# Attention over head pairs: the next pair's four query chunks in steps 0, 2, 4 and 6 instead of 0 to 3

## The reference

```python
q = (x @ wq).reshape(b, s, H, QH).transpose(0, 2, 1, 3)
q_nope, q_pe = (q[..., :NOPE], q[..., NOPE:])
...
q_pe = _rope(q_pe, cos, sin)
qs = jnp.concatenate([q_nope, q_pe], axis=-1)
ks_ = jnp.concatenate([k_nope, jnp.broadcast_to(k_pe, (b, H, s, ROPE))], axis=-1)
scores = jnp.einsum('bhqd,bhkd->bhqk', qs, ks_) * scale
scores = jnp.where(causal, scores, jnp.finfo(scores.dtype).min)
attn = jax.nn.softmax(scores, axis=-1)
out = jnp.einsum('bhqk,bhkd->bhqd', attn, v)
```

## Time and profile before

| | |
|---|---|
| median of 3 runs | 1463.27 us (1458.16 to 1464.06) |
| profiled execution: time, span | 1465.05 us, 1463.3 us |
| mean granted TensorE clock | 0.919 |
| busy over the span | PE 1235.1, POOL 1043.6, DVE 744.3, ACT 700.5 us |

### The profile page before, as it was taken

The page is one execution under the profiler, slowest core; times in us unless marked ns, Lnnn a source line. Parts: engine busy times, 40 slices in busy tenths (PEclk is TensorE's granted clock), DMA queues, the critical chain, the costliest instruction groups (busy, mean ns, idle before and its releaser), DMA issues. The chain is left out here.

```text
span 1463.3 us, 19068 instructions
## 1 busy us (share of the span) xinstructions
PE 1235.1 (84%) x5880; PEld 894.6 (61%) x5881; DVE 744.3 (51%) x1423; ACT 700.5 (48%) x1197; POOL 1043.6 (71%) x764
## 2 busy tenths in 40 slices
PE   6974699999992489988998897689889988998797
PEld 5863455555552356666666666556667666766686
DVE  4578522222224456544655464646546555563557
ACT  3221223333230356676667664246767676666242
POOL 2025768888874578888889876668988898876554
PEclk9986699999995689999999999879999999999999
DMA  9358345455555000000000000000000000002001
GB/s 326 116 157 210 97 62 83 79 79 81 80 75 166 8 8 8 8 1 8 8 8 1 0 1 12 8 8 8 2 7 8 8 8 1 0 1 60 5 8 51
DMA packets 66511, 68.30 MB, mean 47 GB/s; under 512 B 15072, under 2 KB 59680, under 8 KB 66304
## 3 DMA queue, kind: packets, MB, share of 16 engines
q1 hardware_dynamic: 48336, 43.42, 10.0%
q0 software_dynamic: 15168, 20.72, 9.1%
q10 hardware_dynamic: 2928, 3.15, 0.7%
HBM read 46.17 MB, written 21.10 MB: 46 GB/s over the span
## 5 line engine op out<-in xcount | busy, mean ns | idle before, releaser
L1531 POOL TENSOR_TENSOR att_prob_lo<-att_prob,att_prob_hi 128x1024 fp32r<-128x1024 f32 (+1 forms) x160 | 346.2, 2164 | 118.6 <-ACT att_prob_hi L1456 118.5
L1572 DVE TENSOR_REDUCE att_peak<-all_bank 128x1 f32<-128x512 f32 (+3 forms) x384 | 209.3, 551 | 245.4 <-PE all_bank L1343 175.8
L1359 PE MATMUL all_bank<-att_q_hl,sequence_k_hl 128*128 128x512 f32 (+1 forms) x960 | 267.9, 390 | 0.0
L1382 PE MATMUL all_bank<-att_prob_hi,sequence_v_hl 128*128 128x512 f32 (+1 forms) x640 | 212.9, 415 | 61.4 <-POOL att_prob_lo L1531 46.7
L1449 ACT ACTIVATE att_prob<-all_bank 128x1024 f32<-128x1024 f32 (+1 forms) x160 | 150.6, 941 | 156.8 <-PE all_bank L1365 155.0
L1359 PEld LDWEIGHTS all_bank<-att_q_hl,sequence_k_hl 128*128 128x128 f32 x960 | 175.0, 197 | 27.9
L1340 PE MATMUL all_bank<-sequence_k_hl,att_q_hl 128*128 128x512 f32 (+3 forms) x384 | 174.3, 457 | 5.7 <-DVE att_peak L1572 5.3
L1382 PEld LDWEIGHTS all_bank<-att_prob_hi,sequence_v_hl 128*128 128x128 f32 x640 | 113.1, 201 | 78.0 <-POOL att_prob_lo L1531 51.7
L1456 ACT CAST att_prob_hi<-att_prob 128x1024 fp32r<-128x1024 f32 (+1 forms) x160 | 154.2, 964 | 5.1
L916 PE MATMUL all_bank<-early_w_gu,moe_xgT 128*128 x316 | 148.8, 553 | 3.5 <-issue 2.4
L881 POOL DMA_INDIRECT sums<-moe_y,early_slot_far x79 | 125.5, 1588 | 36.4 <-issue 20.4
(11 more groups left out here) (246 smaller groups left out, 2164.2 us busy)
## 6 DMA issues: line engine op xcount, KB each, us to landing
sequence_w_raw<-wqk_rows SPq DMA_DIRECT2D x16, 256.0 KB, 2.6
early_w_gu<-in_gate SPq DMA_DIRECT2D x16, 224.0 KB, 5.5
early_w_gu<-in_up SPq DMA_DIRECT2D x16, 224.0 KB, 6.0
early_w_down<-in_down SPq DMA_DIRECT2D x1, 3584.0 KB, 19.6
sums<-early_zero SPq DMA_DIRECT2D x18, 128.0 KB, 3.7
all_xT<-in_xT SPq DMA_DIRECT2D x4, 512.0 KB, 8.5
all_x_tok<-in_x SPq DMA_DIRECT2D x1, 2048.0 KB, 16.4
x_rows<-all_x_tok SPq DMA_DIRECT2D x4, 512.0 KB, 3.0
```

The costliest lines, as they stand in the source:

```text
L1359: nc.tensor.matmul(ps, k_hl[:, ks, j * P:(j + 1) * P], q_hl[n % 2][:, qs, :, i * BW + q0:(i + 1) * BW], start=g == 0, stop=False)
L1382: mm = nc.tensor.matmul(out, v_hl[:, vs, j, :], part[:, u % 3, half * WIDE:half * WIDE + 2 * w].rearrange("p (h m) -> p h m", h=2), start= ...
L1531: nc.gpsimd.tensor_tensor(prob_lo[:, u % 3, 0:w], prob[:, u % 2, 0:w], prob_hi[:, u % 3, 0:w].bitcast(F32), ALU.subtract).then_inc(lo_sb, 1)
L1572: nc.vector.tensor_reduce(peak[:, n % 2, part, t // 2, h, t % 2:t % 2 + 1], piece_ps[y % 2][:, 0:w], AX_X, ALU.max).then_inc(peak_sb, 1)
```

## The change

The query chunks of the next pair stand in steps 0, 2, 4, 6. So that each piece still comes after its query chunk, the pair leaves 8 of its 24 pieces (not 3) to its own steps 0 to 3, and does 16 of the next pair's, in steps 4 to 9. The splitting of the weights moves from steps 4 and 5 to 7 and 8, DVE's `invert` and POOL's `product` move by a step or more, and the product of a pair's third block moves to step 0 of the next pair.

```diff
-    NEXT_PIECES = [0, 0, 1, 2, 3, 3, 3, 3, 3, 3]
-    OWN_PIECES = [2, 1] + [0] * (NG - 2)
-    FIRST_PIECES = [3, 3, 2] + [0] * (NG - 3)
-    EARLY = NP - sum(FIRST_PIECES)
-    INVERT_AT = {1: (-1, 0), 2: (-1, 1), 3: (0, 0), 4: (0, 1), 5: (1, 0), 6: (1, 1), 7: (2, 0), 8: (2, 1)}
-    PRODUCT_AT = {3: -1, 5: 0, 7: 1, 9: 2}
+    QUERY_AT = {0: 0, 2: 1, 4: 2, 6: 3}
+    NEXT_PIECES = [0, 0, 0, 0, 1, 3, 1, 3, 4, 4]
+    OWN_PIECES = [2, 3, 2, 1] + [0] * (NG - 4)
+    EARLY = NP - sum(OWN_PIECES)
+    INVERT_AT = {0: [(-1, 0)], 1: [(-1, 1)], 3: [(0, 0), (0, 1)], 5: [(1, 0)], 7: [(1, 1)], 8: [(2, 0)], 9: [(2, 1)]}
+    PRODUCT_AT = {0: -2, 2: -1, 4: 0, 8: 1}
...
-                    made = n + 1 < PAIRS and x < QC
+                    made = n + 1 < PAIRS and x in QUERY_AT
...
-                        q_high(n + 1, x)
+                        q_high(n + 1, QUERY_AT[x])
                     if x in last_of:
                         sums(n, last_of.index(x))
-                    if x == 4 and n + 2 < PAIRS:
+                    if x == 7 and n + 2 < PAIRS:
                         weights_high(n + 2)
...
-                        if 1 <= x <= QC:
-                            q_low(n + 1, x - 1)
-                        if x < QC:
-                            rotate(n + 1, x)
+                        if x - 1 in QUERY_AT:
+                            q_low(n + 1, QUERY_AT[x - 1])
+                        if x in QUERY_AT:
+                            rotate(n + 1, QUERY_AT[x])
...
+                product(PAIRS * NB - 2)
```

More of the change, by code:

```diff
@@ L1253, in phase_attention @@
     block_needs = [1 + max(y for y in range(NP) if pieces[y][0] // 2 == i) for i in range(NB)]
-    NEXT_PIECES = [0, 0, 1, 2, 3, 3, 3, 3, 3, 3]
-    OWN_PIECES = [2, 1] + [0] * (NG - 2)
-    FIRST_PIECES = [3, 3, 2] + [0] * (NG - 3)
-    EARLY = NP - sum(FIRST_PIECES)
-    INVERT_AT = {1: (-1, 0), 2: (-1, 1), 3: (0, 0), 4: (0, 1), 5: (1, 0), 6: (1, 1), 7: (2, 0), 8: (2, 1)}
-    PRODUCT_AT = {3: -1, 5: 0, 7: 1, 9: 2}
+    QUERY_AT = {0: 0, 2: 1, 4: 2, 6: 3}
[4 more added lines that the diff above has]
+    PRODUCT_AT = {0: -2, 2: -1, 4: 0, 8: 1}
     def aside(n, x):
[L1264 to L1267, removed]
+        out = [("query", n + 1, QUERY_AT[x])] if n + 1 < PAIRS and x in QUERY_AT else []
+        out += [("piece", n, EARLY + sum(OWN_PIECES[:x]) + a) for a in range(OWN_PIECES[x])]
         if n + 1 < PAIRS:
@@ L1484, in _ @@
                     n, x, _, _ = at(u)
-                    made = n + 1 < PAIRS and x < QC
+                    made = n + 1 < PAIRS and x in QUERY_AT
                     if made:
-                        swap(n + 1, x)
+                        swap(n + 1, QUERY_AT[x])
                     if u + AHEAD < STEPS:
@@ L1546, in _ @@
                     if n + 1 < PAIRS:
-                        if 1 <= x <= QC:
-                            q_low(n + 1, x - 1)
-                        if x < QC:
-                            rotate(n + 1, x)
+                        if x - 1 in QUERY_AT:
+                            q_low(n + 1, QUERY_AT[x - 1])
+                        if x in QUERY_AT:
+                            rotate(n + 1, QUERY_AT[x])
                     if u + AHEAD < STEPS:
                         low(u + AHEAD)
-                    if x == 5 and n + 2 < PAIRS:
+                    if x == 8 and n + 2 < PAIRS:
                         weights_low(n + 2)
@@ L1616, in _ @@
                         beside(item)
-                    if x in INVERT_AT:
-                        i, half = INVERT_AT[x]
+                    for i, half in INVERT_AT.get(x, ()):
                         if n * NB + i >= 0:
```

## The result

The changed kernel takes 1467.38 us (median of 20 runs, 1459.56 to 1475.14), the kernel before on the same chips 1461.39 us (20 runs, 1452.17 to 1464.23). The ratio is **1.0044 [1.0024, 1.0064]**: no gain, but a small loss. The forecast was 1453, with a range of 1437 to 1467. The profiled execution took 1467.2 us with a span of 1465.4 and a mean granted clock of 0.924.

The account below looks back on a forecast made before the run. PE sets the pace, held up in two gaps per middle pair by `sums`. Gains of 22.1 + 1.0 - 0.6 = 22.5 us, less 12.0 for clock drops, net 10.5: 1453 us as run median, range 1437 to 1467.

Parts of the forecast that it names:

- what holds PE up: Middle pairs: gaps of 0.62 us (step 1) and 3.35 (step 3) wait for `sums`, behind `q_high` on ACT.
- Rival (e): Step 3's gap doesn't move because POOL's `low` was its cause: 1477 us, chance 0.03.
- what step 2 gains: Without `q_low` ahead of step 2's rotation, `values` of step 3 starts 2.01 us sooner; its gap becomes 1.9.
- the same chain behind it: Step 0's chain from query to `values` of step 1 stays; only cover goes, so step 1's gap becomes 1.9 us.
- the moved `invert` costs nothing: DVE: moved `invert` priced at nothing, since DVE has 21 us free in a pair and it is read steps later.
- the old loss of 1.71 goes: Middle pairs: the 1.71 us lost to the lower clock behind step 3's gap is gained if new gaps keep the clock.
- The terms for steps 2 to 9: Per middle pair: step 2 gains 2.01 us; steps 4 to 9 lose 2.80 to two queries, gain 0.92 from fewer piece columns.
- a sign of being wrong: Among the listed signs against the forecast: PEclk of 0.5 behind step 1's gap.
- The edge that I took between 1.98 and 2.12 us: Gap length at which the clock falls: 1.98 us kept it, 2.12 lost it; gaps of about 1.9 lie there.
- first and last pairs: First pairs gain 0.5 us each; last pairs lose 0.3 each, idle PE taking most of 1.15 us of added pieces.
- (a) to (c): No gap loses the clock, 1441 (0.26); every step 3 gap does, 1465 (0.18); both of each pair, 1485 (0.05).
- (d): POOL becomes the bound from step 4 on, step 0's query waiting for the weights: about 1467 us, chance 0.10.

Follow-up runs that it names:

- the reduction: Changed kernel with ACT's `sums` ahead of `q_high`, and `att_whole` as a reduction over one operand instead of a maximum of two: 1416.47 us, 0.9688 of the kernel before.
- the run with its gap filled: Kernel before with nine thrown-away matmuls of 512 columns ahead of `values` in step 3: 1442.14 us, 0.9873 of the kernel before.
- the fastest kernel: Changed kernel with `sums` ahead of `q_high`, `att_whole` as a reduction, and own pieces 3, 3, 2 in steps 0 to 2: 1416.04 us, 0.9683.
- the kernel with step 1's gap filled: Changed kernel with six thrown-away matmuls of 512 columns ahead of `values` in step 1: 1462.84 us, 1.0007 of the kernel before.

## Why the prediction was wrong

**Right: what holds PE up.** Both gaps wait for `sums` behind `q_high`, and the view's releaser for step 3, POOL's `low`, was misleading. With `sums` ahead of `q_high` both gaps of the changed kernel fall below 0.5 us and its time goes from 1.0044 to 0.9742 of the kernel before, `low` being untouched. Rival (e) falls.

**Right: what step 2 gains.** From `values` of step 1 to that of step 3 it was 596.89 - 584.33 = 12.56 us before and is 787.51 - 777.01 = 10.50 in the undisturbed pair: 2.06 sooner, where 2.01 was forecast. The step 3 gap is 1.79, where 1.9 was.

**Failed: that step 0 keeps "the same chain behind it", and that the moved `invert` costs nothing.** Step 0's own chain, on which both gaps rest, grew. From the query to `values` of step 1 it was 584.33 - 576.20 = 8.13 us and is 728.59 - 720.13 = 8.46. DVE, then POOL, in the changed kernel at that place:

```profile
719.88 0.16 DVE L1580 TENSOR_TENSOR att_whole<-att_peak 128x4 f32<-128x4 f32 x1
720.08 2.78 DVE L1584 SCALAR_TENSOR_TENSOR att_minus<-all_bf,att_whole 128x512 bf16<-128x512 bf16 x1
722.78 0.94 DVE L1595 RECIPROCAL att_rden<-att_den 128x128 f32<-128x128 f32 x1
723.64 0.62 DVE L1571 TENSOR_REDUCE att_peak<-all_bank 128x1 f32<-128x512 f32 x1
724.18 0.67 DVE L1565 TENSOR_TENSOR all_xT<-all_bank,sequence_cst_turned 128x512 f32<-128x512 f32 x1
```

```profile
719.89 2.40 POOL L1529 TENSOR_TENSOR att_prob_lo<-att_prob,att_prob_hi 128x1024 fp32r<-128x1024 f32 x1 [0.40 <-ACT att_prob_hi L1454]
723.15 1.29 POOL L1503 TENSOR_TENSOR all_xT<-all_xT,sequence_cst_turned 128x512 f32<-128x512 f32 x1 [0.85 <-ACT all_xT L1427]
724.93 1.28 POOL L1506 TENSOR_TENSOR all_xT<-all_xT 128x512 f32<-128x512 f32 x1 [0.49 <-DVE all_xT L1565]
```

The moved pieces bring the third block's maximum to this place. `att_whole` finds POOL free (0.16 us), then `att_minus` starts at 720.08, when POOL's `low` is running until 722.29, and takes 2.78 us; before, all 14 behind an `att_whole` in 540 to 860 us took 0.69. In the changed kernel the 13 there average 1.97. Behind it stands the moved `invert` (0.94), then a peak, and so `by_cos` ends only at 724.85. POOL's second rotation needs it and stands idle for 0.49; 0.33 of that arrive at `values`, whose gap is 2.2 and not 1.9. Putting the `invert` back gave these 0.33 back in the profile, so that part is shown. That `att_minus` is long by POOL's `low` is argued from the rows; the same wait is shown for `att_whole`, by the reduction. The step failed by looking at DVE's 21 free us, which are a sum over the pair: what counted was its queue over the 5 us ahead of `by_cos`, and that its instructions can wait for POOL's.

**Mis-sized: "the old loss of 1.71 goes".** An undisturbed pair is 46.91, forecast 46.14, 0.77 longer. The chain is 0.33 of it. Most of the rest, 0.4, is this term: by the granted clock a drop in the kernel before cost 1.71 us, by the run with its gap filled 1.3. Why it cost less than the granted clock makes of it stays open. The terms for steps 2 to 9, 2.01 - 2.80 + 0.92 = 0.13, held: with the `invert` put back and no drop the changed kernel's pair is 46.58, the filled one's of before 46.66. The new row of waits is small: pieces in step 8 wait 0.3 us for a peak (0.29 at 714.12; the forecast was no gap over 0.5, and one of 12 is 0.6). By the rows DVE takes them late behind another `att_minus`; that wasn't tried by itself.

**Near in number, by luck, and wrong in place: the clock.** I gave nine drops, half of the 14 gaps of step 3 and two in the first pairs. There are 10, but seven stand behind step 1's gap in the middle pairs, which the prediction had named as a sign of being wrong. That I gave none for that gap rested on its coming out below 2 us; the longer chain made it 2.2. Step 3's 1.79 lost nothing in the middle pairs. The edge that I took between 1.98 and 2.12 us isn't there: gaps of 2.20 to 2.22 kept the clock five times, one of 1.79 in a first pair lost it. The 2.12 stood in a stretch where PE was busy for 0.52 of 2.50 us, and so said little of a gap in dense work. The price of a drop: a pair with one is 48.4 to 48.5 us long for 46.9, so 1.5 to 1.6, where 1.71 was used (48.8 in one that also waits 0.3 us longer for a peak).

**Mis-sized: first and last pairs.** First pairs were to gain 0.5 each and lost 1.62 and 0.28. The last two pairs of a batch together went from 78.7 to 81.5 us; about 2.2 of it is the last pair, forecast 0.3. Its idle PE was to swallow most of 1.15 us of added pieces; yet PE's gaps there are as long as before (2.8 us in sum), so the pieces came on top. The other us stays open.

In sum the attention phases were to be 10.5 us shorter and are 5.4 longer: of these 15.9, about 11 come from the middle pairs (12 x 0.77 from the chain and the old loss, and one drop more), 1 from the first, 4 from the last. The whole profiled execution differs by less, 2.2 us; the stages outside attention make up for the rest.

**The rivals.** (a) to (c) didn't come true: 10 of the 28 gaps lost the clock, not none, 14 or more. (d): POOL didn't become the bound in the changed kernel, and no query of step 0 waited for the weights; the 0.49 us at 724.93 is POOL waiting for DVE. (d) does come near in the fastest kernel, at 41.93 of 44.30.

Deeper lies one fact that the prediction had in its terms but didn't draw together. Each pair pays 4 us in two gaps, and the change moved 2 us of cover from step 1 to the steps behind the gaps, while it took 2 us of wait out of step 3: 3.97 became 4.01. Without the clock the sum itself left only 0.13 us per pair, which the 0.33 of waits on DVE took; all the rest of the forecast gain was the clock, at a price that was 0.4 too high.

## What to carry to other kernels

Moving work away from a wait also takes its cover away; add up all gaps of the period before and after, and look first at what stands ahead of the late instruction in its own queue: moving four copies ahead of one gained 2.0% in the kernel before and 3.0 points in the changed one, where re-placing pieces and four chunks gained nothing. An engine's free time over a period says little of a moved instruction; look at who reads behind it in the next few us, and whether what runs ahead of it can be stretched by another engine. Where a shared resource is suspected, the same result by an instruction that doesn't use it is a clean test.

## What was not expected of the hardware

The length of a gap alone doesn't decide whether the clock falls. Gaps of 2.2 us in the same place and between the same matmuls lost it in 7 of 12 middle pairs of the changed kernel and kept it in the others; 1.9 us did much the same with the `invert` put back (8 of 12); 1.79 never lost it in the middle pairs there, and 1.80 did in half of them in the kernel with step 1's gap filled. Two gaps of 2.45 in the first pairs with chunks in steps 0, 1, 4 and 6 kept it. In none of the profiles did a gap of 1.75 us or less in the attention phases lose it, and one of 3.3 in the kernel before always did. What decides in between isn't shown by these runs. The Trainium skill's page "TensorE: Matmul & The Clock Gate", section "A second HAM failure mode: psum-queue depth-cycling", has the clock swing where short idle spells recur between groups of matmuls. The traces agree in that such spells do it, but most of those near 1.8 us did not.

A DVE instruction with two operands in SBUF can last as long as what POOL is doing: 0.16 us became 2.07, which the reduction shows, and 0.69 became 2.78, which is read from the rows. They show it as busy time and not as a wait.
